# A one-core attention and mixture-of-experts kernel: another order of VectorE's work in the output projection, a second buffer of turned rows, and the last stage inside the experts' program

## The reference

```python
x = L0_attn_x                                   # (1, 2048, 512)
x = _layernorm(x + attention(x))                # 16 query heads, 4 key heads, width 128; then @ Wo + bo
logits = x @ router_weight.T                    # 64 experts
probs = softmax(logits); topw, topi = top_k(probs, 8); topw /= sum(topw)
flat_e = topi.reshape(-1)
pos = cumsum(one_hot(flat_e), axis=0)[row, flat_e] - 1      # place of a token in its expert's list
xe = zeros((64, 256, 512)).at[flat_e, pos].set(repeat(x, 8), mode='drop')
g, u = split(einsum('ech,ehf->ecf', xe, gate_up_proj), 2)   # 192 each
ye = einsum('eci,eih->ech', silu(g) * u, down_proj)
y = sum over the 8 choices of topw * ye[flat_e, pos]        # 0 where pos >= 256
out = _layernorm(x + y)
```

## Time and profile before

| | |
|---|---|
| median of three runs | 2180.68 us (2179.51 to 2182.07) |
| the profiled execution | 2180.33 us, span 2178.5 us |
| PE busy | 2044.0 us (94%) |
| DVE busy | 1675.8 us (77%) |
| ACT busy | 1361.8 us (63%) |
| POOL busy | 814.9 us (37%) |
| Wo stage, first to last heads | about 1377 to 1600 us of the span |
| experts | about 1620 to 2123 us |
| last stage | 2137 to 2178.5 us |

### The profile page before, as it was taken

How to read it: one execution, slowest core, us unless ns; L and a number is a source line. 1 busy time by engine, 2 the same in 40 slices (tenths; PEclk the granted TensorE clock), 3 DMA queues, 4 the chain that set the end, 5 groups by cost and what they waited for, 6 DMA issues and landing times. The chain is left out here.

```text
span 2178.5 us, 41238 instructions
## 1 busy us (share of the span) xinstructions
PE 2044.0 (94%) x13409; PEld 1808.9 (83%) x13409; DVE 1675.8 (77%) x3503; ACT 1361.8 (63%) x2735; POOL 814.9 (37%) x792
## 2 busy tenths in 40 slices
PE   8999989999999999999999999899959999999990
PEld 6888878988888988899888898677748999999980
DVE  5899987877678776787767876577757888888874
ACT  3677776766667656676666766322327777877761
POOL 1000023332233322332323332133335777787760
PEclk9999999999999999999999999999969999999995
DMA  7558563010520105201062000767637999999987
GB/s 243 184 216 286 215 217 123 34 59 21 183 104 26 59 22 189 98 25 63 18 238 87 25 26 20 264 239 275 232 102 217 296 297 299 303 293 296 298 220 245
DMA packets 140170, 362.60 MB, mean 166 GB/s; under 512 B 16209, under 2 KB 33233, under 8 KB 135377
## 3 DMA queue, kind: packets, MB, share of 16 engines
q1 hardware_dynamic: 111312, 292.09, 37.7%
q0 software_dynamic: 28672, 68.17, 13.2%
HBM read 224.27 MB, written 135.94 MB: 165 GB/s over the span
## 5 line engine op out<-in xcount | busy, mean ns | idle before, releaser
L653 PE MATMUL p_S<-p_kT,p_q 128*128 128x512 f32 (+3 forms) x1920 | 473.6, 377 | 10.6 <-ACT p_prob L729 9.9
L653 PEld LDWEIGHTS p_S<-p_kT,p_q 128*128 128x128 f32 x1920 | 324.2, 190 | 59.0 <-ACT p_prob L729 15.3
L840 POOL TENSOR_SCALAR p_prob<-p_prob,p_inv 128x128 f32<-128x128 f32 (+7 forms) x256 | 191.3, 747 | 457.1 <-DVE p_inv L789 457.1
L840 POOL TENSOR_SCALAR p_prob<-p_prob,p_inv,p_part 128x1024 f32<-128x1024 f32 x128 | 153.0, 1196 | 496.0 <-DVE p_inv L794 496.0
L665 PE MATMUL p_TP<-p_ident,p_prob 128*128 128x128 f32 x2176 | 304.4, 274 | 1.8 <-DVE p_pT1l L800 1.8
L778 DVE TENSOR_REDUCE p_nmax<-p_S 128x1 f32<-128x1024 f32 (+7 forms) x256 | 251.7, 983 | 23.0 <-PE p_S L653 22.0
L665 PEld LDWEIGHTS p_TP<-p_ident,p_prob 128*128 128x128 f32 x2176 | 246.2, 141 | 25.9 <-DVE p_pT1l L800 5.6
L738 ACT CAST p_pT1h<-p_TP 128x512 fp32r<-128x512 f32 (+3 forms) x320 | 154.7, 526 | 152.9 <-PE p_TP L665 152.7
L738 ACT CAST p_pT0h<-p_TP 128x512 fp32r<-128x512 f32 (+3 forms) x320 | 155.2, 526 | 151.9 <-PE p_TP L665 150.6
L686 PE MATMUL p_O<-p_pT0h,p_v 128*128 128x256 f32 x1088 | 227.5, 293 | 6.0 <-DVE p_pT0l L800 6.0
L686 PE MATMUL p_O<-p_pT1h,p_v 128*128 128x256 f32 x1088 | 226.7, 293 | 6.2 <-issue 3.8
(11 more groups left out here) (221 smaller groups left out, 4507.4 us busy)
## 6 DMA issues: line engine op xcount, KB each, us to landing
p_w_raw<-in_gu SPq DMA_DIRECT2D x64, 768.0 KB, 6.9
qk_scratch<-p_qout SPq DMA_DIRECT2D x80, 512.0 KB, 2.7
p_q<-qk_scratch SPq DMA_DIRECT2D x16, 2048.0 KB, 9.2
o_scratch<-p_oT SPq DMA_DIRECT2D x128, 256.0 KB, 2.3
p_ot<-o_scratch SPq DMA_DIRECT2D x32, 1024.0 KB, 7.0
p_w_raw<-in_gu SPq DMA_DIRECT2D x64, 256.0 KB, 8.3
...
```

The source lines that it names most:

```text
L653: mm = nc.tensor.matmul(out, x, y, start=(n == 0), stop=(n == 2))
L840: nc.gpsimd.tensor_scalar(prob[k][:, cols], prob[k][:, cols], inv[:, k:k + 1], scale, ALU.mult, ALU.mult).then_inc(normed, 1)
```

## The change

- DVE's order in the Wo stage becomes `normalise(b)`, `place(b-1)`, (`weights_lo`), `choose(b)`, `mark(b-1)`. `residual` moves to POOL, ahead of its comparisons. TURN and ROUTE become 6 and 8; TABLE and SUM stay 12 and 14.
- For the last two blocks the one-hot matrices are divided otherwise: of block 14 DVE makes 4 `hi_hot` (before `choose(15)`), and POOL 4 `hi_hot` and 8 `lo_hot`; of block 15 DVE makes 3 `lo_hot` and 8 `hi_hot`, POOL 5 `lo_hot`.
- `xT` gets two buffers, and ACT's copy waits for `gate_up(e-2)`. For the first expert PE does a third of `gate_up(0)`, then `turn(1)`, then the rest.
- `stage_finish` joins `mixture`'s block. The even sum comes in two transfers of 2 MB, the odd one in eight of 512 KB, the output leaves in eight. Groups are of two blocks; POOL adds the second block of each, and ACT makes all outputs but the last. DVE's instructions are linked one to the next by a semaphore.

```diff
-            TURN, ROUTE, TABLE, SUM = 7, 9, 12, 14
+            TURN, ROUTE, TABLE, SUM = 6, 8, 12, 14
...
-            def residual(b, k, n):
-
-                dve.wait_ge(xr_in[k], n * 16 + 16)
-                nc.vector.tensor_tensor(xb[k][:], xr[k][:], bo_b[:], ALU.add).then_inc(biased, 1)
-
...
-                link(nc.vector.tensor_scalar(number[:], number[:], float(P), None, ALU.add))
                 if not early:
                     dve.wait_ge(lo_ready, b)
+                link(nc.vector.tensor_scalar(number[:], number[:], float(P), None, ALU.add))
...
-            def mark(b, early):
+            def mark(b, early=False, his=range(TOPK), los=()):
 
                 dve.wait_ge(placed, b + 1)
                 if not early:
                     dve.wait_ge(tabled, b)
-                for n in range(TOPK):
+                for n in los:
+                    nc.vector.tensor_scalar(lo_hot[:, n, :], iota_lo[:], lo[:, n:n + 1], None, ALU.is_equal)
+                for n in his:
                     ins = nc.vector.tensor_scalar(hi_hot[:, n, :], iota_lo[:], hi[:, n:n + 1], number[:], ALU.is_equal,
                                                   ALU.mult)
                 ins.then_inc(hi_ready, 1)
 
-            def step(i, first, last=False, end=False):
+            def step(i, first, last=False):
                 for k in range(2):
                     b = i * 2 + k
-                    after = not (first and k == 0)
-                    if after:
+                    normalise(b, k, i, first)
+                    if not (first and k == 0):
                         place(b - 1, 1 - k, first)
-                    normalise(b, k, i, first)
-                    if not (end and k == 1):
-                        residual(b + 1, 1 - k, i + k)
-                    if after:
-                        mark(b - 1, first)
                     if last:
                         weights_lo(dve, b)
                     choose(b, k, i, first)
-
-            residual(0, 0, 0)
+                    if not (first and k == 0):
+                        mark(b - 1, first)
+
             step(0, True)
             with dve.Fori(1, NB // 2 - 2) as i:
                 step(i, False)
             step(NB // 2 - 2, False, last=True)
-            step(NB // 2 - 1, False, last=True, end=True)
+            normalise(NB - 2, 0, NB // 2 - 1, False)
+            place(NB - 3, 1, False)
+            weights_lo(dve, NB - 2)
+            choose(NB - 2, 0, NB // 2 - 1, False)
+            mark(NB - 3)
+            normalise(NB - 1, 1, NB // 2 - 1, False)
+            place(NB - 2, 0, False)
+            mark(NB - 2, his=range(DVE_HIS))
+            choose(NB - 1, 1, NB // 2 - 1, False)
             place(NB - 1, 1, False)
-            mark(NB - 1, False)
+            mark(NB - 1, los=range(POOL_LOS, TOPK))
             dve.wait_ge(tabled, NB)
...
+            def residual(b, k, n, early):
+
+                wait_alone(pool, passed, xr_in[k], n * 16 + 16)
+                if not early:
+                    wait_alone(pool, passed, normed, b - 1)
+                nc.gpsimd.tensor_tensor(xb[k][:], xr[k][:], bo_b[:], ALU.add).then_inc(biased, 1)
+
+            def mark(b, early, los=range(TOPK), his=()):
+
+                wait_alone(pool, passed, placed, b + 1)
+                if not early:
+                    wait_alone(pool, passed, tabled, b)
+                for n in his:
+                    nc.gpsimd.tensor_scalar(hi_hot[:, n, :], iota_lo[:], hi[:, n:n + 1], number[:], ALU.is_equal, ALU.mult)
+                for n in los:
+                    ins = nc.gpsimd.tensor_scalar(lo_hot[:, n, :], iota_lo[:], lo[:, n:n + 1], None, ALU.is_equal)
+                ins.then_inc(lo_ready, 1)
+
             def step(i, first):
-                for k in range(2):
-                    b = i * 2 + k
-                    wait_alone(pool, passed, placed, b + 1)
-                    if not (first and k == 0):
-                        wait_alone(pool, passed, tabled, b)
-                    for n in range(TOPK):
-                        ins = nc.gpsimd.tensor_scalar(lo_hot[:, n, :], iota_lo[:], lo[:, n:n + 1], None, ALU.is_equal)
-                    ins.then_inc(lo_ready, 1)
-
-            loop(pool, NB // 2, step)
+                residual(i * 2 + 1, 1, i, first)
+                mark(i * 2, first)
+                residual(i * 2 + 2, 0, i + 1, False)
+                mark(i * 2 + 1, False)
+
+            residual(0, 0, 0, True)
+            step(0, True)
+            with pool.Fori(1, NB // 2 - 1) as i:
+                step(i, False)
+            residual(NB - 1, 1, NB // 2 - 1, False)
+            mark(NB - 2, False, his=range(DVE_HIS, TOPK))
+            mark(NB - 1, False, los=range(POOL_LOS))
...
-        xT = [sb(f"xT{s}", [P, NC, CAP], F32R, kb=1 + 4 * (s == "l")) for s in "hl"]
+        xT = [[sb(f"xT{k}{s}", [P, NC, CAP], F32R, kb=(1, 130)[k] + 4 * (s == "l")) for s in "hl"] for k in (1, 0)][::-1]
...
-            gate_up(0)
+            gate_up(0, range(1))
             turn(1)
+            gate_up(0, range(1, 3))
...
-                    if e >= 1:
-                        act.wait_ge(gated, e)
-                    nc.scalar.copy(xT[HI][:, :, c * P:(c + 1) * P], tp[c][:]).then_inc(x_hi, 1)
+                    if e >= 2:
+                        act.wait_ge(gated, e - 1)
+                    nc.scalar.copy(xT[e % 2][HI][:, :, c * P:(c + 1) * P], tp[c][:]).then_inc(x_hi, 1)
...
+    def sync(sp):
+        sp.wait_ge(added[0], 16 * CH * (E // 2))
+        for g in range(0, NG, 4):
+            sp.dma_start(blocks(even, g, 4), rows(sum_d[0], g, 4)).then_inc(even_in, 16)
+        sp.wait_ge(added[1], 16 * CH * (E // 2))
+        for g in range(NG):
+            sp.dma_start(blocks(odd, g), rows(sum_d[1], g)).then_inc(odd_in[g], 16)
+        for g in range(NG):
+            sp.wait_ge(act_done, GROUP * g + (GROUP if g < NG - 1 else 1))
+            if g == NG - 1:
+                sp.wait_ge(dve_done, 1)
+            sp.dma_start(rows(out, g), blocks(res, g)).then_inc(res_out, 16)
+        sp.wait_ge(res_out, 16 * NG)
+
...
+        def statistics(g):
+            b = g * GROUP
+            dve.wait_ge(odd_in[g], 16)
+            link(nc.vector.tensor_tensor(total[:, b, :], even[:, b, :], odd[:, b, :], ALU.add))
+            link(nc.vector.bn_stats(st[:, b, :], total[:, b, :]))
+            nc.vector.bn_aggr(mv[:, b, :], st[:, b, :]).then_inc(var_ready, 1)
+            dve.wait_ge(joined, g + 1)
+            link(nc.vector.bn_stats(st[:, b + 1, :], total[:, b + 1, :]))
+            nc.vector.bn_aggr(mv[:, b + 1, :], st[:, b + 1, :]).then_inc(var_ready, 1)
+
+        def scales(g):
+            cols = slice(g * GROUP, (g + 1) * GROUP)
+            dve.wait_ge(sd_ready, g + 1)
+            link(nc.vector.reciprocal(rstd[:, cols], sd[:, cols]))
+            nc.vector.scalar_tensor_tensor(shift[:, cols], mv[:, cols, 0], -1.0, rstd[:, cols], ALU.mult, ALU.mult
+                                           ).then_inc(shift_ready, 1)
...
+    def gpsimd(pool):
+        pool.wait_ge(even_in, 16 * 2)
+        for g in range(NG):
+            b = g * GROUP + 1
+            pool.wait_ge(odd_in[g], 16)
+            nc.gpsimd.tensor_tensor(total[:, b, :], even[:, b, :], odd[:, b, :], ALU.add).then_inc(joined, 1)
```

176 lines of the change are left out of this document (77 added, 99 removed).

## The result

The changed kernel takes 2264.19 us (median of four runs, 2263.82 to 2268.94) against 2180.73 for the kernel before in the same comparison: ratio 1.0385, 95% interval 1.0371 to 1.0400. It is 83.5 us slower; the forecast was 63.3 us more than the median. The profiled span is 2262.4 us (before 2178.5).

What follows compares the result with a forecast made beforehand. The prediction took PE to bound the Wo stage, with almost no slack on DVE. From 2180.3 us, +46.5 (order), +20 (clock), -1.8 (seam) and -1 (last stage) gave 2244, range 2220 to 2262.

Steps and rivals of the forecast that it cites:

- The order: Wo stage: DVE's new order makes PE wait 3.45 us at each table, +3.1 a turn, 46.5 us in all.
- `residual` on POOL ... Zero: Wo stage: the addition moved to POOL may cost 2 us there but stays hidden, so zero.
- such a hold: Last stage, rival: POOL's additions hold DVE's, 0.7 us for each of eight, +5.6, so 2250; chance 0.06.
- The clock: Wo stage: PE's granted clock falls after each of 14 table waits, 1.4 us each, +20; bounds 0 and +35.
- each fall lasts longer: Wo stage, rival: the clock gets little time to rise between waits, 35 for 20, so 2259; chance 0.12.
- The seam: Between Wo stage and experts: two `xT` buffers let SiLU start 1.8 us earlier, -1.8; bounds -3.5 and 0.
- The last stage: `stage_finish`: earlier additions and a smaller last store, less losses in links and ACT's queue, -1; bounds -5 and +6.
- All three terms: Last stage: first additions 1.4 us earlier, last store 1.3 less, some 1.7 lost in links and ACT's longer queue.

Runs made afterwards that it cites:

- Experiment 5: Changed kernel with 16 more matmuls, whose result nothing reads, ahead of each table of the Wo loop: 2238.74 us, ratio 1.0265.
- experiment 6: Changed kernel with PE taking the table of b-3 after head 3 of block b, DVE's order kept: 2177.00 us, ratio 0.9981.
- experiment 3: Changed kernel with `residual` back on DVE behind `mark`, so that POOL only compares: 2246.14 us, ratio 1.0302.
- experiment 8: Changed kernel with the Wo stage of before, and POOL's additions in the last stage made by DVE: 2178.15 us, ratio 0.9989.
- experiment 9: Changed kernel with the Wo stage of before, and SiLU's table loaded early by one more ACT instruction: 2173.36 us, ratio 0.9965.
- experiment 7: Kernel before with the new last stage alone, its Wo stage, single `xT` buffer and experts' start kept: 2176.62 us, ratio 0.9982.

## Where the prediction held, and which steps failed

The direction and the main mechanism were right: PE waits at a table whose place was not moved. The time, 2264.2, is 20 us over the forecast and lies 2 us above the range: 13.3 from a term that was put at zero, 11.3 from the clock, less 4.7 from the last stage, which came out better than forecast and hid part of the miss.

- **The order: +46.5 forecast, 46.8 by the division.** The agreement to 0.3 is in part luck (1.1 of it lies ahead of the stage, and the three last turns were 1.4 shorter than forecast), but every part is within 1.5. Experiment 5 confirms it without the clock (17.55 a turn, 16.5 and 1.02 for `mark`), experiment 6 by taking the table out of the way.
- **"`residual` on POOL ... Zero": wrong, 13 us.** I costed the addition on POOL's own queue, where it is hidden indeed, at up to 2 us (it took 1.26). I did not ask what DVE does at that moment. It fell into `mark`, the one instruction group of DVE that PE waits for, and its hold came out at the table (experiment 3; some 1.6 of the 13 us are holds by POOL's comparisons). I named such a hold only for the last stage, where it was worth about 1.6 us (experiment 8). The sign was in the earlier trace rows: in the kernel before the 16 longest of POOL's 128 comparisons (797 to 1320 ns, median 601) all overlap the `residual` addition on DVE. I read that spread for the last stage and did not ask what the same two engines would do in the Wo stage once the addition changed sides. This is the failed step that put the result outside.
- **The clock: +20 forecast, 31.3.** The chance of falls was right (all 14 turns), the price of one was taken from a single row, 1.70, less what might hide. It was 2.2 on average and between 1.2 and 2.8, so the second failed step is the size of this term. By the rule of the page "TensorE: Matmul & The Clock Gate" of the Trainium skill ("HAM oscillation") every turn would pay, and the trace agrees. It lies inside the bounds (0 to 35), but together with the 13 us it needed the rival "each fall lasts longer", at 0.12. Part of the clock's 31 may follow from the first error: with the wait shorter by `mark`'s hold, the clock cost 27.0 (experiment 3), though the same code with the hold gave 31.3 and 29.5.
- **The seam: -1.8 forecast, -1.4 by the trace, -2.0 by the times.** The nearness is luck. The term was a shorter wait of PE, and that shrank by 0.6 only, since the table load of 1.28 us that I counted as hidden was not; experiment 9 gives it back. The rest of the -1.4 is a higher clock in `gate_up(0)`, and the -2.0 is not resolved (experiment 7).
- **The last stage: -1 forecast, -5.7 by the trace, -5.0 by the times.** All three terms were off the same way. The first addition came 2.1 us earlier and not 1.4. The last store took 2.2 us less and not 1.3 (from the end of ACT's last output to the end of the span 3.9, before 6.1). And in place of a loss of 1.7 up to the end of ACT's last output there was a gain of 1.4: a pair took 2.8 us of DVE and not 3.1 (the eight first additions start between 2234.04 and 2253.59: 19.55 / 7), since POOL ran ahead and DVE seldom waited for it. By the trace it is just outside its bound of -5.
- **The range.** With 13 us at zero and without a bound, its upper end had no room for a hold and long falls at once.
